# One RWKV-style layer in fp32 on one core: the last sequence by halves of 128 tokens, with new orders for five passes and more

## What is computed

```python
xn = _ln(x, ln1_w, ln1_b)
sx = _token_shift(xn, state[:, i1])              # previous token minus this one
xxx = jnp.tanh((xn + sx * maa_x) @ maa_w1)       # then @ maa_w2, five mixes
x5 = xn[:, :, None] + sx[:, :, None] * (maa_stack + xxx)
w = jnp.exp(-jnp.exp(time_decay + jnp.tanh(x5[:, :, 1] @ decay_w1) @ decay_w2))
r, k, v = x5[:, :, 3] @ Wr.T, x5[:, :, 0] @ Wk.T, x5[:, :, 2] @ Wv.T
g = jax.nn.silu(x5[:, :, 4] @ Wg.T)
def step(s, rkvw):
    a = k_t[:, :, :, None] * v_t[:, :, None, :]
    out = jnp.einsum('bhk,bhkd->bhd', r_t, u * a + s)
    return (a + w_t[:, :, :, None] * s, out)
att = group_norm(outs) * gn_w + gn_b             # 32 heads of 16 channels
x = x + att * g @ Wo.T
xn2 = _ln(x, ln2_w, ln2_b)
sx2 = _token_shift(xn2, state[:, i0])
rr = jax.nn.sigmoid((xn2 + sx2 * ffn_maa_r) @ ffn_Wr.T)
kk = jnp.square(jax.nn.relu((xn2 + sx2 * ffn_maa_k) @ ffn_Wk.T))
x = x + rr * (kk @ ffn_Wv.T)
```

## Time and profile before

| | |
|---|---|
| time, median of 3 runs | 750.32 us (746.72 to 753.39) |
| the profiled execution | 749.5 us, of which the span is 747.7 us |
| TensorE busy | 687.3 us, 92% of the span |
| VectorE busy | 531.5 us, 71% |
| GpSimd busy | 395.1 us, 53% |
| ScalarE busy | 314.9 us, 42% |
| starts of `c_fk`, one a pass (L883) | 129.6, 215.8, 300.8, 386.6, 471.4, 556.7, 646.8, 719.8 us |

### The profile page before, as it was taken

The page is one execution under the profiler, slowest core; times in us unless marked ns, Lnnn a source line. Parts: engine busy times, 40 slices in busy tenths (PEclk is TensorE's granted clock), DMA queues, the critical chain, the costliest instruction groups (busy, mean ns, idle before and its releaser), DMA issues.

```text
span 747.7 us, 17273 instructions
## 1 busy us (share of the span) xinstructions
PE 687.3 (92%) x7260; PEld 473.1 (63%) x7260; DVE 531.5 (71%) x799; ACT 314.9 (42%) x611; POOL 395.1 (53%) x223
## 2 busy tenths in 40 slices
PE   5898698998999999999999999999999899995777
PEld 4785575567675686657774676657875577753453
DVE  4738875698469876788658876788765975699441
ACT  2171444139432564229522573418632284225211
POOL 1247743776458546576457566565657553472100
PEclk9998799999999999999999999999999999999789
DMA  6900000001000200002000200002000010000000
GB/s 204 406 10 12 26 3 0 3 29 65 2 1 1 93 3 2 3 2 93 2 1 1 92 4 1 1 1 94 3 0 1 23 43 3 29 1 2 3 28 28
DMA packets 13135, 24.61 MB, mean 33 GB/s; under 512 B 3840, under 2 KB 5632, under 8 KB 12032
## 3 DMA queue, kind: packets, MB, share of 16 engines
q1 hardware_dynamic: 13056, 23.47, 9.1%
HBM read 18.35 MB, written 4.19 MB: 30 GB/s over the span
## 4 chain that ended last, share of the span: by engine, by line
PE 59%; DVE 13%; issue 10%; POOL 9%; DMA 4%; SPq 3%; ACT 1%; POOLq 0%; DVEq 0%; ACTq 0%
PE FB L591 22%; PE FA L883 8%; PE BAB L865 7%; PE FB L599 5%; POOL pp L506 5%; PE BAB L842 3%; DMA pp<-x 3%; PE FA L670 3%; PE BAB L769 2%; POOL wide L548 2%; PE FA L906 2%; PE BAB L582 2%; POOL mixes L459 1%; DVE st L1185 1%; DVE half L1380 1%
## 5 line engine op out<-in xcount | busy, mean ns | idle before, releaser
L468 POOL TENSOR_TENSOR mixes<-mixes 128x1024 f32<-128x1024 f32 x30 | 81.2, 2706 | 121.0 <-ACT mixes L1019 121.0
L506 POOL TENSOR_TENSOR pp<-rT,kT 128x2048 f32<-128x2048 f32 (+1 forms) x32 | 109.0, 3414 | 47.6 <-DVE rT L1284 43.8
L470 POOL TENSOR_TENSOR mixes<-mixes,xnT 128x1024 f32<-128x1024 f32 x30 | 75.8, 2528 | 2.4
L1364 DVE TENSOR_TENSOR half<-BAB,vp 128x2048 f32<-128x2048 f32 x23 | 52.7, 2290 | 14.4 <-PE BAB L769 13.6
L883 PE MATMUL FA<-wide,fk_s 128*128 128x256 f32 x256 | 59.8, 394 | 2.5 <-DVE wide L1545 2.4
L1380 DVE TENSOR_REDUCE half<-half 128x256 f32<-128x2048 f32 (+2 forms) x30 | 61.0, 2034 | 0.6
L591 PE MATMUL FB<-mixes,wv_s 128*128 128x256 f32 x256 | 61.0, 387 | 0.2 <-issue 0.2
L591 PE MATMUL FB<-mixes,wk_s 128*128 128x256 f32 x256 | 60.6, 390 | 0.3 <-ACT wT L992 0.3
L591 PE MATMUL FB<-mixes,wg_s 128*128 128x256 f32 x256 | 60.3, 384 | 0.1
L906 PE MATMUL FA<-fv_s,wide 128*128 128x512 f32 x128 | 59.6, 609 | 0.0
L599 PE MATMUL FB<-fr_s,wide 128*128 128x512 f32 x128 | 58.8, 602 | 0.0
(11 more groups left out here) (174 smaller groups left out, 1333.6 us busy)
## 6 DMA issues: line engine op xcount, KB each, us to landing
pp<-x SPq DMA_DIRECT2D x8, 512.0 KB, 4.7
xt<-x SPq DMA_DIRECT2D x8, 512.0 KB, 4.3
out<-wide SPq DMA_DIRECT2D x7, 512.0 KB, 3.1
half<-wv SPq DMA_DIRECT2D x1, 1024.0 KB, 4.9
wk_s<-wk SPq DMA_DIRECT2D x1, 1024.0 KB, 7.3
wr_s<-wr SPq DMA_DIRECT2D x1, 1024.0 KB, 8.4
wg_s<-wg SPq DMA_DIRECT2D x1, 1024.0 KB, 10.4
wo_s<-wo SPq DMA_DIRECT2D x1, 1024.0 KB, 13.5
```

The costliest lines, as they stand in the source:

```text
L468: nc.gpsimd.tensor_tensor(slot, slot, sx, ALU.mult).then_inc(s_["mixm_ready"], 1)
L470: nc.gpsimd.tensor_tensor(slot, slot, xnT[:, :, 1:L + 1], ALU.add).then_inc(s_["mix_ready"], 1)
L506: ins = nc.gpsimd.tensor_tensor(pp[:, i % 2, 0:size].rearrange("p (n i j) -> p n i j", i=m, j=m), spread(r.unsqueeze(3), 3, m), spread(k.u ...
L1364: nc.vector.tensor_tensor(product_of(b, i).rearrange("p (n i j) -> p n i j", i=m, j=m), BAB[:, :].rearrange("p (n i j) -> p n i j", i=m, j=m),
```

## The change

For the last sequence, from the group norm on, each step works on a half of 128 tokens: `b_gnh`, `b_norm2h`, `c_fkh` and `b_xrh` stand for `b_gn`, `b_norm2`, `c_fk` and `b_xr`; `transpose_half` signals each half; `b_wo` of that sequence is one half per part, 8 and 8 records; `relu` and square go by halves of tokens. The buffers of these steps (`xn2T_end`, `sx2_end`, `xk_end`, `xr_end`, `x1_end`, and `sq_end` for `rr`) share nothing with those of sequence 6, so that `b_wo` waits no more for `out_ready` and `b_norm2` no more for `stored`; the last `c_mul` waits for `stored` instead, before it writes `outt`. `c_mul` and `c_out` of sequence 6 stand between the steps of sequence 7, `c_fv1` of sequence 6 between the two `b_norm2` steps. The last pass has an order of its own, `final`. Besides, the orders of `main`, `end` and `last` are new on all four engines. The passes `first` and `second` are unchanged.

```diff
--- before.py
+++ after.py
         main="""
-            c_fk b_score0 c_fr0 b_score1 c_fv0 b_g0 b_score2 c_fr1 b_score3 f_norm b_g2 b_g1 b_score4 c_fv1
-            f_lora0 f_lora1 b_vtok f_m20 b_g3 b_ktok f_m21 b_kv0 f_dec1 b_kv1 f_dec2 f_m22 b_acc f_k0 f_k1
-            f_k2 b_apply0 b_apply1 f_k3 b_apply2 b_apply3 f_v0 f_v1 f_m23 f_v2 b_gn0 b_gn1 f_m24 f_v3 b_wo0
+            c_fk b_score0 c_fr0 b_score1 c_fv0 b_score2 b_g0 c_fr1 b_score3 b_g1 f_norm b_g2 b_score4 c_fv1
+            f_lora0 f_lora1 b_vtok b_ktok f_m20 b_g3 f_m21 b_kv0 b_kv1 f_dec1 f_dec2 f_m22 b_acc f_k0 f_k1
+            f_k2 b_apply0 b_apply1 f_k3 b_apply2 b_apply3 f_m23 f_v0 f_v1 f_v2 b_gn0 f_m24 b_gn1 f_v3 b_wo0
             b_wo1 f_r0 f_r1 b_norm20 b_norm21 f_r2 f_r3""".split(),
         end="""
-            c_fk b_score0 f_norm c_fr0 b_score1 b_g0 b_g1 c_fv0 b_score2 c_fr1 b_score3 c_fv1 b_score4 b_g2
-            b_g3 f_lora0 f_lora1 b_vtok f_m20 f_m21 b_ktok f_dec1 b_kv0 b_kv1 f_dec2 f_m22 b_acc f_k0 f_k2
-            f_m23 f_k1 b_apply0 b_apply1 f_k3 b_apply2 f_v0 b_apply3 f_v1 f_m24 f_v2 f_v3 b_gn0 b_gn1 f_r0
-            b_wo0 b_wo1 f_r2 f_r1 b_norm20 b_norm21 f_r3""".split(),
+            c_fk b_score0 f_norm c_fr0 b_score1 c_fv0 b_score2 c_fr1 b_score3 b_g0 c_fv1 b_score4 b_g1 b_g2
+            b_vtok f_lora0 f_lora1 b_ktok f_m20 b_g3 f_m21 b_kv0 b_kv1 f_dec1 f_dec2 f_m22 b_acc f_k0 f_k1
+            b_apply0 b_apply1 f_m23 f_k2 b_apply2 b_apply3 f_k3 f_v0 f_v1 f_v2 f_v3 f_m24 b_gn0 b_gn1 f_r0
+            b_wo0 b_wo1 f_r1 f_r2 b_norm20 b_norm21 f_r3""".split(),
         last="""
-            c_fk b_score0 c_fr0 b_score1 b_g0 c_fr1 b_score2 b_g1 b_g2 b_score3 b_g3 b_score4 b_vtok c_fv0
-            b_ktok b_kv0 b_kv1 b_acc b_apply0 b_apply1 b_apply2 b_apply3 c_fv1 b_gn0 b_gn1 b_wo0 b_wo1
-            b_norm20 b_norm21""".split()),
+            c_fk b_score0 c_fr0 b_score1 c_fr1 b_score2 b_g2 b_g0 b_g1 b_score3 b_g3 b_vtok b_score4 c_fv0
+            b_ktok b_kv0 b_kv1 b_acc b_apply0 b_apply1 b_apply2 b_apply3 b_gn0 b_gn1 b_wo0 b_wo1 b_norm20
+            c_fv1 b_norm21""".split(),
+        final="""
+            c_fkh0 c_fr0 c_fr1 c_fkh1 c_fv0 c_fv1""".split()),
...
         main="""
-            b_step1 b_mul0 b_step2 b_mul1 b_red1 b_step4 c_mul0 b_mul2 b_red2 b_mul3 b_red3 b_mul4 f_xin
-            c_mul1 b_step8 b_red4 f_mix0 b_gate0 n_stats b_gate1 b_kvx0 b_kvx1 b_kv b_scan b_exp b_var1
-            b_var0 b_root b_nrm0 b_nrm1 b_gn b_wo0 b_wo1 b_xhat20 b_xhat21 n_norm b_norm2 b_xr""".split(),
+            b_step1 b_mul0 b_step2 b_mul1 b_red1 b_step4 b_mul2 c_mul0 b_red2 b_mul3 b_red3 b_mul4 f_xin
+            b_step8 c_mul1 b_red4 b_gate0 f_mix0 b_kvx1 b_gate1 b_kvx0 n_stats b_kv b_scan b_exp b_var0
+            b_var1 b_root b_nrm0 b_nrm1 b_gn n_norm b_wo0 b_wo1 b_xhat20 b_xhat21 b_norm2 b_xr""".split(),
         end="""
-            b_step1 b_mul0 b_step2 b_mul1 b_step4 b_gate0 b_red1 b_mul2 b_red2 b_mul3 b_red3 f_xin b_mul4
-            b_step8 c_mul0 c_mul1 b_red4 f_mix0 b_gate1 b_kvx0 b_kvx1 b_kv b_scan b_exp b_var0 b_var1 b_root
-            b_nrm0 b_nrm1 b_gn b_wo0 b_xhat20 b_wo1 b_xhat21 b_norm2 b_xr""".split(),
+            b_step1 b_mul0 b_step2 b_mul1 b_red1 b_step4 b_mul2 b_red2 b_mul3 c_mul0 b_red3 b_mul4 f_xin
+            b_gate0 b_step8 c_mul1 b_red4 f_mix0 b_gate1 b_kvx1 b_kvx0 b_kv b_scan b_exp b_var0 b_var1
+            b_root b_nrm0 b_nrm1 b_gn b_wo0 b_wo1 b_xhat20 b_xhat21 b_norm2 b_xr""".split(),
         last="""
-            b_prodx b_step1 b_mul0 b_step2 b_mul1 b_step4 b_red1 b_mul2 b_gate0 b_red2 b_mul3 b_gate1 b_red3
-            b_mul4 b_step8 b_red4 b_ktok b_kvx0 b_kvx1 b_kv b_scan b_exp b_var0 b_var1 b_root b_nrm0 b_nrm1
-            b_gn c_mul0 c_mul1 b_wo0 b_wo1 b_xhat20 b_xhat21 b_norm2 b_xr""".split()),
+            b_prodx b_step1 b_mul0 b_step2 b_mul1 b_red1 b_step4 b_mul2 b_red2 b_gate0 b_mul3 b_gate1 b_red3
+            b_mul4 b_step8 b_red4 b_ktok b_kvx0 b_kvx1 b_kv b_scan b_exp b_var0 b_var1 b_root b_nrm0 c_mul0
+            b_nrm1 b_gnh0 b_gnh1 b_wo0 b_xhat20 b_wo1 b_xhat21 b_norm2h0 b_xrh0 b_norm2h1 c_mul1 b_xrh1""".split(),
+        final="""
+            c_mul0 c_mul1""".split()),
...
         main="""
-            b_prod0 b_prod1 b_prod2 b_prod3 b_prod4 b_add1 c_out0 f_sx c_out1 b_add2 b_s0 b_add3 b_add4
-            f_mix1 f_mix2 f_mix3 f_mix4 b_wo0 b_wo1 n_stats""".split(),
+            b_prod0 b_prod1 b_prod2 b_prod3 c_out0 b_prod4 f_sx b_s0 c_out1 b_add1 b_add2 b_add3 b_add4
+            f_mix1 f_mix2 n_stats f_mix3 f_mix4 b_wo0 b_wo1""".split(),
         end="""
-            b_prod0 b_prod1 b_prod2 b_prod3 b_add1 b_prod4 b_add2 b_s0 b_add3 f_sx c_out0 c_out1 b_add4
+            b_prod0 b_prod1 b_prod2 b_prod3 b_s0 b_add1 b_prod4 f_sx c_out0 b_add2 c_out1 b_add3 b_add4
             f_mix1 f_mix2 f_mix3 f_mix4 b_wo0 b_wo1""".split(),
         last="""
-            b_prod0 b_s0 b_prod1 b_prod2 b_prod3 b_prod4 b_add1 b_add2 b_add3 b_add4 c_out1 c_out0 b_wo0
-            b_wo1""".split()),
+            b_prod0 b_prod1 b_prod2 b_prod3 b_prod4 b_add1 b_add2 b_add3 b_add4 b_s0 c_out0 b_wo0 b_wo1
+            c_out1""".split(),
+        final="""
+            c_out1 c_out0""".split()),
...
         main="""
-            c_fk0 c_fk1 c_fr0 c_fr1 f_norm b_rcopy f_lora0 b_g0 f_lora1 b_vtok b_ktok f_mix1 b_decays b_g1
-            f_dec1 b_kv1 b_kv0 f_dec2 f_mix2 b_exp f_k0 f_k1 b_sq0 b_sq1 f_mix3 b_gn f_v0 f_v1 f_mix4
+            c_fk0 c_fk1 c_fr0 c_fr1 f_norm f_lora0 f_lora1 b_g0 b_vtok b_ktok f_mix1 b_g1 b_decays f_dec1
+            b_kv0 b_kv1 f_dec2 b_rcopy f_mix2 b_exp f_k0 b_sq0 b_sq1 f_k1 f_v0 f_mix3 b_gn f_v1 f_mix4
             b_norm2 f_r1 f_r0""".split(),
         end="""
-            c_fk0 c_fk1 f_norm c_fr0 b_g0 c_fr1 b_decays b_g1 f_lora0 f_lora1 b_vtok b_ktok f_mix1 f_dec1
-            b_rcopy b_kv1 b_kv0 f_dec2 f_mix2 b_exp f_mix3 f_k0 b_sq0 b_sq1 f_k1 f_v0 b_gn f_mix4 f_v1
-            b_norm2 f_r0 f_r1""".split(),
+            c_fk0 c_fk1 f_norm c_fr0 c_fr1 b_g0 b_decays b_rcopy f_lora0 f_lora1 b_vtok b_ktok f_mix1 b_kv0
+            b_g1 f_dec1 b_kv1 f_dec2 f_mix2 b_exp f_mix3 f_k0 b_sq0 b_sq1 f_k1 f_v0 b_gn f_mix4 f_v1 f_r0
+            b_norm2 f_r1""".split(),
         last="""
-            c_fr0 c_fk0 c_fr1 b_g0 c_fk1 b_g1 b_vtok b_rcopy b_ktok b_kv0 b_kv1 b_decays b_exp b_sq0 b_sq1
-            b_gn b_norm2""".split()),
+            c_fk0 c_fr0 c_fr1 c_fk1 b_g0 b_g1 b_vtok b_ktok b_rcopy b_decays b_kv0 b_kv1 b_exp b_sq0 b_sq1
+            b_gnh0 b_gnh1 b_norm2h0 b_norm2h1""".split(),
+        final="""
+            c_fk0 c_fr0 c_fk1 c_fr1""".split()),
 )
...
+        xn2T_end = half[:, 0:C * (L + 1)].rearrange("p (c l) -> p c l", c=C)
+        sx2_end = half[:, C * (L + 1):C * (2 * L + 1)].rearrange("p (c l) -> p c l", c=C)
+        xk_end = half[:, C * (2 * L + 1):C * (3 * L + 1)].rearrange("p (c l) -> p c l", c=C)
+        xr_end = mixes[:, 0, :, :]
+        x1_end = vexp_end[:, 1]
...
             run(None, at(B - 1), at(B - 2), at(B - 3), order["end"])
             run(None, None, at(B - 1), at(B - 2), order["last"])
-            run(None, None, None, at(B - 1))
+            run(None, None, None, at(B - 1), order["final"])
...
+            def transpose_half(dst, src, t, ready):
+                for c in range(C):
+                    ins = nc.tensor.transpose(dst[:, t * E + c * P:t * E + (c + 1) * P],
+                                              src[:, t, c * P:(c + 1) * P], ident_s[:])
+                ins.then_inc(ready, 1)
...
+                        for q in range(C):
+                            if q % 2 == 0:
+                                pe.wait_ge(s_["y_ready"], C * b + 2 * part + q // 2 + 1)
+                            ins = nc.tensor.matmul(BA[:, part * E:(part + 1) * E], yb_end[:, q, part * P:(part + 1) * P],
+                                                   big["wo"][:, q, :], start=(q == 0), stop=(q == C - 1))
+                        ins.then_inc(s_["wo_ready"], 1)
+                        return
                     for q, t in (((0, 0), (0, 1), (1, 0), (1, 1), (2, 0), (3, 0)), ((2, 1), (3, 1)))[part]:
                         if t == 0:
...
+            def c_fkh(t):
+                def run(b, par, n):
+                    pe.wait_ge(s_["mul_ready"], T * b - 1 + t)
+                    for q in range(C):
+                        pe.wait_ge(s_["xk_ready"], C * b + C * t + q + 1)
+                        for c in range(C):
+                            ins = nc.tensor.matmul(FA[:, t * E + c * P:t * E + (c + 1) * P],
+                                                   big["fk"][:, q, c * P:(c + 1) * P], xk_end[:, q, t * P:(t + 1) * P],
+                                                   start=(q == 0 and c == 0), stop=(q == C - 1), skip_group_check=True)
+                    ins.then_inc(s_["fk_ready"], 1)
+                return run
...
+            def b_gnh(t):
+                def run(b, par, n):
+                    act.wait_ge(nrmh_ready, t + 1)
```

(52 more changed lines are left out.)

66 lines of the change are left out of this document (43 added, 23 removed).

## The result

| | before | after |
|---|---|---|
| median of 20 runs each | 747.1 us (744.76 to 753.39) | 752.86 us (750.41 to 756.79) |
| span of the profiled execution | 747.7 us | 751.1 us |
| starts of `c_fk` (L918 after) | 129.6, 215.8, 300.8, 386.6, 471.4, 556.7, 646.8 | 129.8, 218.7, 304.3, 392.3, 477.7, 564.8, 654.4 |

The ratio is 1.0067, 95% interval 1.0049 to 1.0086: 0.7% slower, where 744.5 us and faster was the forecast, and outside the range of 738 to 751.5. By stages the two profiled executions differ in opposite ways: the five `main` passes take 435.0 us for 427.2 (+7.8), `end` 89.6 for 90.1 (-0.5), and from the start of `last` on 96.7 for 100.9 (-4.2).

The account below looks back on a forecast made before the run. TensorE, busy 92% of the span, was taken to bound the kernel, with the tail a chain. From 749.5 us it took off 3.9 (tail), 1.0 (`main`) and 0.1 (`end` and `last`): 744.5 us, range 738 to 751.5.

Parts of the forecast that it names:

- the term of 1.0 us less in `main`: Five `main` passes: the new orders take 1.0 us off in all, with 1 us per pass to either side.
- the early `n_norm`: `main`, VectorE: the norm ahead of `b_wo0` takes away 0.6 us of wait at one pass's first `xk`.
- The tail, by its steps: Last sequence from the group norm on: a followed chain of half steps, ending at 739.7 against 743.7; 3.9 us less taken.
- The term that decided, the narrow matmuls: `c_fkh0` and `c_fkh1` in the tail: 0.11 us a record, 3.5 us a half, bounds 3.5 to 7.1.
- the rival that prices them as wide ones: Tail: narrow matmuls at 0.22 us a record make it 7.1 us longer, 751.6 us; chance 0.06.
- Item 4 of the chain: Tail: `c_fkh0` starts at 718.75, 1.1 us earlier than the 719.84 of before, at full clock.
- `end` and `last`: Passes six and seven's new orders: `end` net 0, within 2 us; `last` net 0.1 us less, within 1.5.
- `c_out1` beside the reduce at 1.3 us: `main`, POOL: `c_out1`, now beside VectorE's reduce, ends at 423.2 against 422.65; it took 2.39 us before.
- `f_dec2` off the load: `main`, TensorE: its gate no longer waits for the load; starts 0.4 us sooner, about 0.8 us of wait left.
- the orders cost: Rival, `main` and `end`: `c_mul1` behind `b_step8` makes later steps 1.1 us late a pass, 6.6 us, 751; chance 0.14.
- The orders pay: Rival, `main` and `end`: a third to two thirds of 15 us idle goes, 737 to 742 us; chance 0.20.
- The halves do little: Rival, tail: low clock through `b_wo1` and pauses leave a gain of 0 to 2, 746.5 to 748.5 us; chance 0.12.

Follow-up runs that it names:

- e2: The kernel before with only the four new orders of `main`, one for each engine; 756.67 us, ratio 1.013.
- e8: The kernel before with one TensorE move in `main`: `f_dec1` behind `b_kv1` instead of between `b_kv0` and `b_kv1`; 748.61 us, ratio 0.9999.
- e7: e1 with one VectorE move in `main`: `b_gate1` ahead of `n_stats` instead of behind it; 758.63 us, ratio 1.013.
- e11: e1 with, in `last` on TensorE, `c_fv1` of sequence 6 ahead of `b_gn0` instead of between `b_norm20` and `b_norm21`; 744.63 us, ratio 0.9966.
- e1: The kernel after with the orders of `main` and `end` put back on all four engines, halves kept; 744.45 us, ratio 0.9962.
- e4: The kernel after with `n_norm` on VectorE in `main` one step earlier, ahead of `b_gn`; 746.93 us, ratio 1.0009.
- e13: The kernel after with one GpSimd move in `main`: `f_mix4` behind `b_wo1` instead of ahead of `b_wo0`; 756.45 us, ratio 1.0112.
- e15: The kernel after with VectorE's and GpSimd's orders of `main` put back, TensorE's and ScalarE's new ones kept; 748.79 us, ratio 1.0009.
- e9: e5 with one more VectorE move in `main`: `b_gate1` ahead of `b_kvx1`; 761.3 us, ratio 1.0171.
- e3: The kernel after with `n_norm` on VectorE in `main` again behind `b_xhat21` instead of ahead of `b_wo0`; 748.22 us, ratio 1.0018.
- e5: e4 with `f_dec1` again between `b_kv0` and `b_kv1` in `main` on TensorE; 756.08 us, ratio 1.0109.
- e6: e5 with, besides, `f_m23` on TensorE in `main` ahead of `b_apply1` instead of behind `b_apply3`; 763.94 us, ratio 1.0185.

## Why the prediction was wrong

The step that failed is the term of 1.0 us less in `main`. It priced the early `n_norm` at the 0.5 us an instruction that it took with GpSimd idle. In its new place an instruction took 2.54 us beside GpSimd's mix, and that made most of the 7.8 us that `main` lost.

**The tail, by its steps.** Right in the steps from `c_fkh0` on, and partly by luck in the number. The sum said 3.9 us, the two profiled executions give 4.2. The order of the steps came out as followed through: `b_wo0` to the end without a pause, `c_fv1` in the gap, `c_fkh0` behind it at full clock. The term that decided, the narrow matmuls, was 3.5 us for a half; start to start they took 3.6, so the rival that prices them as wide ones falls. By the ratio that the Trainium skill gives ("TensorE: Matmul & The Clock Gate", section "Back-to-back issue gap") they would have taken 5.1 us, an estimate; the measurement, 3.6, decides against it. Too small was `b_wo` after the pause: 9.19 us for 8.80, with the clock up only at 716.8. Item 4 of the chain, `c_fkh0` 1.1 us earlier than `c_fk`, holds against that one execution of before only: in e2 and e8, whose tail is that of before, `b_wo` took 7.11 us and `c_fk` followed the start of `last` by 71.1 us, where `c_fkh0` followed by 71.6. What stands is the part behind it: from there to the end 25.1 us in 12 of the 14 kernels with halves (25.5 in e7, 26.7 in e11), for 27.6 to 27.9 without them. The tails of e2 and e8 took 98.6 and 99.0 us, so against them the tail gains 1.9 to 2.3 us, not 4. e1 against before, 3.2 us by medians of that comparison, lies between. Part of what is missing is `c_fv1`: ahead of `b_gn0` (e11) it had the clock up for `b_wo`, which then took 7.10 us instead of 9.2, but the empty norm gap cost as much again.

**`end` and `last`.** Right within the ranges: -0.5 in `end`.

**`main`.** This is where it failed: -1.0 forecast, +7.8 measured, in passes of 85.4 to 88.9 us. By its lines:
- The early `n_norm` takes away the 0.6 us of wait at the first `xk` of one pass: that wait went, but I took the norm at the 0.5 us it had in an idle neighbourhood, and did not look at what GpSimd does at the time of its new place. It met `f_mix4` in all five passes, lasted 5.0 us for 1.0, and held `b_wo0`'s sum and so `b_norm2` back. e4 prices it at 4 to 6 us of the time, 5.6 in the main passes; e13 shows the cause. In the prediction I had GpSimd's contention at `c_out1` only, and for two-input instructions only.
- `c_out1` beside the reduce at 1.3 us: right, ten of `c_out` take 12.7 us for 18.4. `thR` still in time: wrong in one pass of five, where the issue of its two transfers took SyncE 2.70 us instead of 1.24, and TensorE waited 1.1, then 0.6 for `tk`.
- `f_dec2` off the load, with about 0.8 us of wait left: right, 0.6 a pass, on the gate.
- Nothing in the sum stood for `issue`. It rose by 3.3 us in main. `b_kv0` and `b_kv1` side by side are part of it (e8: +1.1 us), but e8's time did not rise.

The base: the sum started from an execution of 749.5 us, where the median of the 20 is 747.1. Its own terms, taken from 747.1, would have given 742, still further from the measured 752.86.

The rivals: *the orders cost* had the right sign with another mechanism; it named `c_mul1` behind `b_step8`, which made `c_out1` end 0.3 to 0.8 us later in a pass, not 1.1. Its chance of 0.14 was too small for five passes of new orders on four engines of which I priced each step in its old surroundings. *The orders pay* falls; its price was also wrong, since 5 to 10 us off 744.5 give 734.5 to 739.5 and not 737 to 742, and its "five equal waits" were 0.9 to 1.5 us. *The halves do little* (a tail that gives 0 to 2 us) lies closer to the 1.9 to 2.3 us against e2 and e8 than my 3.9, though the pauses that it asked for were not there.

**What stays open**: which moves of TensorE and ScalarE hold the other 2 us of main (e15 only hints that they are there), and what an `issue` pause depends on.

## What to carry to other kernels

Before you move a VectorE instruction, look at what GpSimd runs at its new time, and which of the two starts first; where GpSimd does, price it as what is left of GpSimd's instruction plus a little less than its own duration (0.3 us of 0.53 here). And look at what a removed wait sets free: a transfer, a copy or a GpSimd instruction that now starts earlier can land in front of a VectorE instruction that the path needs (e7 lost 14 us by removing 5). An order is worth something only with its neighbours: the same place of the norm cost nothing in one set of orders and 9 us in the next.

## What the hardware showed that I had not expected

- **VectorE's scale-and-shift of one tensor waits for GpSimd.** 128x512 in fp32 took 0.53 us alone (ten in e13) and 2.54 beside a GpSimd multiply or add (ten in the kernel after), ending 0.3 us behind GpSimd's end; GpSimd was not slowed (2.35 and 2.23 us). In e4 VectorE's row began 0.08 to 0.14 us ahead of GpSimd's; it took 0.54 and GpSimd 0.3 us more. A lead of 0.04 to 0.06 us, as the first norm of each pair has in the kernel after, did not save it. For the instruction with two inputs (L1506) it is the same question: 1.93 us where VectorE began ahead (e1), 3.8 where GpSimd did (e7). The Trainium skill has it so, page "SBUF — State Buffer", section "Who interferes with whom": the two share a pair of ports under an exclusive lock, whoever issues first keeps it for the whole instruction, and a tensor-with-scalar instruction can be of the kind that takes it. The trace agrees, 2.54 us against 0.53.
- **Pauses labelled `issue` can be two things.** In e7 and e9 the first pause at `b_apply` ended 0.1 us behind the spreading that it needed, in each of the five passes. Others end 1.2 to 1.5 us behind a transfer of 16 KB on the queue of kind "instruction": so do all 15 of 0.7 us or more in main of before, after, e1, e3 and e8. Start and end of that transfer, and when TensorE went on, for five of them:

```
kernel   transfer             TensorE goes on   later by
before   184.00 to 184.92     186.45            1.53
after    185.45 to 186.76     188.16            1.40
after    699.64 to 700.59     702.11            1.52
e1       184.16 to 185.29     186.59            1.30
e3       517.52 to 518.45     519.81            1.36
```

  That these are TensorE's own instructions is inferred from the times. Main has 39 or 40 such transfers in each of these executions, most of them without a pause behind them. The pauses fall in stretches of 64 to 128 matmuls of 13 to 18 ns each (`b_kv`, `b_apply`), in `b_apply` at the same place of the program in both rounds of the loop (a round is two passes; the pauses stand in passes 1 and 3).
- **A pause of 1 to 2 us in main can cost more than itself.** In or shortly behind pauses of 1.1 to 2.3 us the granted clock went to half for 3.4 to 10.2 us in e2, e3, e5, e6, e7, e8, e9 and e15. It does so sometimes only. Of the five pauses of 1.6 us at `f_dec2` in e5 three have such a fall and two have none. The same pause of 1.81 us in `b_kv1` of the fifth pass had 10.2 us at half clock in e3, 3.4 in e2 and none in the kernel after (521.3). That this is why the runs of one kernel spread, over 11 us in e3, is inferred.
